# Attention of layer 1: choosing behind the splits, normalising ahead of weighing, rows half a batch sooner

## The reference, cut to what matters

```
x = x + tanh(g_xattn[0]) * L0_attention(layernorm(x), ctx)
x = x + tanh(g_ffn[0])   * L0_experts(layernorm(x))
x = x + tanh(g_xattn[1]) * L1_attention(layernorm(x), ctx)     # 16 heads of 64
x = x + tanh(g_ffn[1])   * L1_prototypes(layernorm(x))
```

## Time and profile before

| | |
|---|---|
| median of 3 runs | 2970.56 us (2968.09 to 2979.39) |
| profiled execution | 2975.93 us |
| its span, first to last instruction | 2973.9 us |
| granted TensorE clock, mean | 0.980 |
| TensorE busy | 2718.9 us, 91% |
| VectorE busy | 2397.3 us, 81% |
| ScalarE busy | 2224.4 us, 75% |
| GpSimd busy | 1998.5 us, 67% |

### The profile page before, as it was taken

One profiled execution on the slowest core, in us unless ns is written; L12 is line 12 of the kernel. 1 busy time (PEld: TensorE's weight loads), 2 busy tenths in 40 slices (PEclk: granted clock), 3 DMA queues, 4 the chain that ended last, 5 costly groups with the idle time before them and its releaser, 6 DMA issues. The chain is left out here.

```text
span 2973.9 us, 95792 instructions
## 1 busy us (share of the span) xinstructions
PE 2718.9 (91%) x31406; PEld 2150.3 (72%) x31406; DVE 2397.3 (81%) x5742; ACT 2224.4 (75%) x5708; POOL 1998.5 (67%) x2649
## 2 busy tenths in 40 slices
PE   3888998699999999969799999999999999999996
PEld 2444444577777777746578888888888888888885
DVE  6788787588888888865588888888888888888884
ACT  2667666578778777755578888888888888888884
POOL 3894000466766766645268888888888888888886
PEclk9999999799999999989999999999999999999998
DMA  5996666233233233533267877777777777777764
GB/s 153 335 365 271 259 277 256 74 87 89 77 91 87 77 90 88 188 130 84 68 141 166 168 161 158 156 154 153 155 155 154 153 153 158 155 154 161 152 140 87
DMA packets 585174, 459.62 MB, mean 155 GB/s; under 512 B 400000, under 2 KB 543984, under 8 KB 571696
## 3 DMA queue, kind: packets, MB, share of 16 engines
q1 hardware_dynamic: 564528, 406.48, 54.6%
q0 software_dynamic: 7328, 23.40, 2.5%
q10 hardware_dynamic: 12960, 25.23, 2.3%
HBM read 235.08 MB, written 148.83 MB: 129 GB/s over the span
## 5 line engine op out<-in xcount | busy, mean ns | idle before, releaser
L389 POOL TENSOR_TENSOR a_probT_lo<-a_expT,a_probT_hi 128x512 f16<-128x512 f32 x256 | 291.4, 1159 | 218.2 <-ACT a_probT_hi L472 218.2
L465 ACT ACTIVATE a_expT<-banks,a_top,w_score_scale 128x512 f32<-128x512 f32 (+1 forms) x384 | 272.3, 709 | 152.7 <-PE banks L556 145.8
L1168 POOL TENSOR_TENSOR a_pn<-a_prob,a_rsum 128x1024 f32<-128x1024 f32 (+1 forms) x256 | 310.3, 1233 | 27.1 <-DVE a_rsum L1555 24.3
L156 PE MATMUL banks<-a_xnT,w_q_hi 128*128 128x256 f16 x1024 | 281.5, 275 | 16.0 <-DMA a_xnT<-a_xn_parts 13.9
L156 PE MATMUL banks<-a_vo_front,a_probT_hi 128*128 128x256 f16 x1024 | 279.3, 273 | 15.0 <-DVE a_probT_lo L1541 12.9
L1250 ACT ACTIVATE a_qT_hi<-banks 128x512 f16<-128x512 f32 x252 | 149.6, 594 | 182.8 <-PE banks L158 182.8
L157 PE MATMUL banks<-a_xnT,w_q_hi 128*128 128x256 f16 x1024 | 281.2, 275 | 0.0
L158 PE MATMUL banks<-a_xnT,w_q_lo 128*128 128x256 f16 x1024 | 281.2, 275 | 0.0
L158 PE MATMUL banks<-a_vo_front,a_probT_lo 128*128 128x256 f16 x1024 | 279.1, 273 | 0.0
L157 PE MATMUL banks<-a_vo_front,a_probT_hi 128*128 128x256 f16 x1024 | 279.1, 273 | 0.0
L1539 DVE TENSOR_TENSOR a_qT_lo<-banks,a_qT_hi 128x512 f16<-128x512 f32 x252 | 173.1, 687 | 73.0 <-ACT a_qT_hi L1250 72.5
(11 more groups left out here) (381 smaller groups left out, 10137.6 us busy)
## 6 DMA issues: line engine op xcount, KB each, us to landing
vo<-kv_vo_out SPq DMA_DIRECT2D x38, 2048.0 KB, 7.7
a_vo_front<-vo SPq DMA_DIRECT2D x128, 512.0 KB
kt<-kv_k_out ACTq DMA_DIRECT2D x9, 2560.0 KB, 15.0
a_k<-kt SPq DMA_DIRECT2D x64, 308.0 KB, 3.6
kv_raw_e<-in_L_ffn_w POOLq DMA_DIRECT2D x16, 1024.0 KB, 9.6
a_x<-in_x SPq DMA_DIRECT2D x64, 256.0 KB
a_y<-in_x SPq DMA_DIRECT2D x64, 256.0 KB, 2.7
x<-a_y SPq DMA_DIRECT2D x64, 256.0 KB, 2.9
```

The lines of the kernel that those rows point to most:

```text
L156: nc.tensor.matmul(out, lhs[0], rhs[0], start=start, stop=False)
L389: pool.tensor_tensor(probT[b][1][:, first:end, :], expT[b][:, first:end, :], probT[b][0][:, first:end, :], ALU.subtract).then_inc(prob_rea ...
L465: act.activation(expT[1 - h][0:rows, first:end, :], bank, ACT.Exp, bias=top[0:rows, 0:1], scale=weights["score_scale"][0:rows, 0:1]).then_ ...
L1168: last = pool.tensor_tensor(keys_of(pn[h]), e[:, :, first:end].rearrange("p (a c) k -> p a c k", a=outer), rsum[h][:, :].rearrange("p (a c ...
```

## The change

Three edits, all in the loop of layer 1.

1. VectorE: `farther_weight`, the picks and `wsel` move from the end of body t to body t+1, right behind its three splits of probabilities; so they are written there for t-7 in place of t-6.
2. GpSimd: `normalise` stands ahead of `weigh`.
3. The rows of a batch are made half a batch sooner. `norm_stats(i+3)` stands in half 1 (it was i+2 in half 0), ScalarE's `norm_log` to `rows_high` of i+2 in half 0 (they were in half 1), `rows_low(i+2)` and `turn_rows(i+2)` in half 1 (they were i+1 in half 0). The first batches get their calls ahead of the loop.

```diff
@@ SP body
-                if h == 0 and live(i + 1, NB):
-                    turn_rows(i + 1, *ahead(u, j, 1))
+                if h == 1 and live(i + 2, NB):
+                    turn_rows(i + 2, *ahead(u, j, 2))
@@ SP, ahead of the loop
+        turn_rows(1, 1, 0)
         bodies(sp, body)
@@ GpSimd body
-                if h == 0 and live(i + 1, NB):
-                    rows_low(i + 1)
+                if h == 1 and live(i + 2, NB):
+                    rows_low(i + 2)
+                if live(t - 2, NT):
+                    normalise(t - 2, h, u)
                 if live(t - 7, NT):
                     weigh(t - 7, 1 - h)
-                if live(t - 2, NT):
-                    normalise(t - 2, h, u)
                 if live(t - 7, NT):
                     weighed_low(t - 7)
@@ GpSimd, ahead of the loop
+        rows_low(1)
         bodies(pool, body)
@@ ScalarE body, the same edit at norm_log, norm_root, norm_shift and:
-                if h == 1 and live(i + 2, NB):
+                if h == 0 and live(i + 2, NB):
                     norm_apply(i + 2, u + 2)
                     rows_high(i + 2, (u + 2) % BODIES, j + (u + 2) // BODIES)
                 prep(3)
@@ VectorE body, behind the splits
+                if live(t - 7, NT):
+                    farther_weight(t - 7)
+                    need(dve, wtops_ready, t - 6)
+                    need(dve, top_ready, t - 6)
+                    for k in range(2):
+                        last = nc.vector.tensor_scalar(pick[:, k, :], const["iota"][:, :], topf[:, k:k + 1],
+                                                       wtop[:, k:k + 1], ALU.is_equal, ALU.mult)
+                    last.then_inc(picked, 1)
+                if live(t - 7, NT):
+                    need(dve, picked, t - 6)
+                    need(dve, hw_lo, t - 7)
+                    nc.vector.tensor_tensor(wsel[:, :], pick[:, 0, :], pick[:, 1, :], ALU.add).then_inc(wsel_ready, 1)
                 if live(t - 6, NT):
                     nearest_two(t - 6)
@@
-                if h == 0 and live(i + 2, NB):
-                    norm_stats(i + 2, (u + 2) % BODIES, j + (u + 2) // BODIES)
+                if h == 1 and live(i + 3, NB):
+                    norm_stats(i + 3, (u + 3) % BODIES, j + (u + 3) // BODIES)
@@ VectorE body, near its end: the same lines for t-6 are taken out
-                if chosen:
-                    farther_weight(t - 6)
...
                 prep(3)
@@ VectorE, ahead of the loop
+        norm_stats(2, 2, 0)
         bodies(dve, body)
```

## The result

The changed kernel takes 3132.78 us (3132.28 to 3138.77, 4 runs) against 2969.32 us of the kernel before: ratio 1.0548, interval 1.0521 to 1.0576. It is 5.5% slower. The forecast was 3146 us with a range of 3060 to 3195, and slower at 0.89.

A forecast was written before the change was run, and what follows sets the result against it. It took TensorE as nearly the bound before, at 22.80 us a batch, then a chain over VectorE, GpSimd and ScalarE at 25.75: +2.95 over 58 batches is +171, with ends +175, giving 3146 us, range 3060 to 3195.

The forecast's parts named there:

- its ring: Per half batch, GpSimd's sums, VectorE's inverse sums, splits and picks, `weigh`, ScalarE's `weighed_high`, GpSimd's low halves and sums: 12.03 to 12.58 us.
- What it removes: TensorE's two waits for VectorE's low halves of probabilities in half 0 go: by itself -0.90 us a batch.
- What edit 1 adds: Late choosing joins one chain over VectorE, GpSimd and ScalarE: 24.6 us a batch over GpSimd against 22.8.
- ScalarE's detour: `norm_apply` and `rows_high`, 1.75 us on ScalarE between q0 and q1 in half 0; that path takes 9.82 us from `wsel`.
- rivals 4 and 5: 4: GpSimd round alone, ScalarE's detour hidden, 24.6 us a batch, 3075 us, chance 0.17; 5: the forecast, 3146 us, 0.55.
- The sum: Half 0 3.9 + 9.82, half 1 3.9 + 8.13: 25.75 us a batch, +2.95; +171 over 58 batches, +175 with ends.
- The shared port: VectorE picks and GpSimd instructions block each other; without that the period would be about 0.9 us shorter.
- The rows made sooner: Row work moved to the other half: nothing at DMA, SP, `rows_low` and `norm_stats`, but 1.75 us on ScalarE.
- the stall's end: Both TensorE waits in half 0 go because inverse sums no longer stand behind the choosing, starting about 1.5 us sooner.
- Rival 1: The stall goes and nothing replaces it: 21.9 us a batch, 2918 us, chance 0.06.
- Rivals 2 and 3: Attention of half 1 waits for the FFN `a_y` bank: 2, about 2966 us, chance 0.04; 3, 2985 to 3030 us, 0.10.
- the bank: Freed by VectorE's FFN `a_y` for TensorE's attention of half 1; its chain was put at 11.0 us, under 12.03.

The follow-up runs named there:

- choose_only: The kernel before with only VectorE's choosing moved behind the splits, `weigh` still ahead of `normalise`: 3165.69 us, ratio 1.0628.
- choose_normalise: The kernel before with the choosing behind the splits and `normalise` ahead of `weigh`, rows made where they were: 3090.19 us, ratio 1.0401.
- after_bank_early: The changed kernel with VectorE's `a_y` of the FFN moved ahead of the choosing in both halves: 3156.99 us, ratio 1.0619 to the kernel before.
- after_rows_behind: The changed kernel with `norm_apply` and `rows_high` moved behind q1's high half, still half 0: 3097.82 us, ratio 1.0418 to the kernel before.
- rows_only: The kernel before with only the rows made half a batch sooner: 2936.07 us, ratio 0.9878.

## Why the prediction was right

Its verdict and its ring held, and most of its sizes, link by link in the batch shown above. The last two halves are medians from 1900 to 2800 us.

| link | predicted | measured after |
|---|---|---|
| inverse sums to `wsel`, half 0 | 3.9 us | 2315.25 - 2311.39 = 3.86 |
| `wsel` to inverse sums of half 1, over ScalarE | 9.82 | 2324.75 - 2315.25 = 9.50 |
| whole batch | 25.75 | 25.48 |
| half 0, inverse sums to inverse sums | 13.72 | 13.28 |
| half 1 | 12.03 | 11.99 |
| GpSimd idle before `weigh` | 0.8 | 0.80 |
| GpSimd idle before the low halves | 0.9 | 0.89 |
| wait for the distances, moved to half 0 | 0.55 | 0.54 |

- **What it removes.** TensorE's waits for low halves went. Right, but the 0.90 us a batch can't be seen here, since TensorE is no longer the bound.
- **What edit 1 adds.** Ring over sums, splits, picks, `weigh`. Shown by choose_only, choose_normalise and after_bank_early.
- **ScalarE's detour.** Shown by after_rows_behind; 35 to 39 us instead of the 71 between rivals 4 and 5. This term was sized too large: `wsel` to the inverse sums took 9.50 us for 9.82, and the round without the detour (choose_normalise, after_rows_behind) took 24.6 to 24.9 us a batch by median against 24.6.
- **The sum.** The steady period was forecast 0.27 us too long, 16 us over 58 batches. What the forecast added for the first batches and the ends (4 us) is nearer 8: 163.5 us measured, less 58 x 2.68. The two errors partly cancel, which is luck of a few us and does not carry the verdict. One sign was off: TensorE was to be near 85% busy and is at 89% in the earlier trace rows's stretch.
- **The shared port.** By the rows, the choosing stands while GpSimd runs: in half 0 of the changed kernel `wtop` takes 0.58 and the picks 0.70 us beside `normalise`, in choose_only 0.15 and 0.51 with GpSimd idle. That lengthens inverse sums to `wsel` from 3.2 to 3.86. The Trainium skill (SBUF — State Buffer, section on who interferes with whom) says that a VectorE instruction with two SBUF inputs, as `wtop` is, contends with a GpSimd instruction that reads SBUF, and one in a two-port mode with any; the second to issue is blocked. The traces agree: `wtop` ends at 2314.19, and so does the first instruction of `normalise` (2312.27 + 1.92).
- **The rows made sooner.** Here a step failed, though the forecast's number does not show it. The prediction had `rows_low`'s move at nothing, and left the stall's end to edit 1. It had itself said that 2.14 us of choosing stood beside `rows_low`, against 1.34 in the other half, but did not carry that to the move: without it rows_only has 0.90 us of choosing, and the whole stall goes for nothing in return. In the changed kernel this gain can't show, since TensorE is no longer the bound. That the error did not reach the sum is luck; it would have reached any advice on which edit to keep.
- **Rival 1's number** (2918, the stall gone and nothing in its place) is nearly what rows_only reaches, 2936 us with TensorE busy 198.32 us in 200 and 21.9 us for most batches. Its mean of 22.3 a batch holds a few longer ones, one of 28.7 us.
- **Rivals 2 and 3**, the bank: refuted as the cause by after_bank_early. That it would be the limit once the ring is cut is neither shown nor refuted.

## What to carry to other kernels

When a step moves behind another on an in-order engine, write down the ring that it closes with all engines and add its links; average idle time of 13 to 16% per engine says nothing about it. TensorE's longest wait in a slower kernel names who came last, not what is slow: pull that producer forward once, and see whether the time follows. When it doesn't, look at single batches beside the mean, with the granted clock of each: a gain and a loss can hide in it. Test each edit of a bundle alone: here one of three was worth 1.2%, and the other two hid it.

## What was not expected of the hardware

The same two picks and their weight took 2.14 us beside GpSimd's `rows_low`, 1.34 beside its sums, and 0.90 with GpSimd idle. In the rows each held instruction ends within 0.05 us of the GpSimd instruction that runs, so the price depends on the length of that single instruction. In the kernel before the first pick of half 0 ends at 2303.76 + 1.10 and `rows_low` at 2304.83:

```profile
2303.76 1.10 DVE L1670 TENSOR_SCALAR a_pick<-iota,a_topf,a_wtop 128x32 f32<-128x32 f32 x1
```

The turning DMA of `hw`, whose landing takes 3.4 us by the median in the changed kernel, had so little slack that low halves 2 us later cost TensorE 1.6 us of waiting a batch. And in about every fourth batch a wait of 2 to 2.8 us for it was followed by some 3 us or more at the lower clock level, although the mean granted clock of the stretch is still 0.98.
